# Layer-norm statistics and their Newton step moved from VectorE to ScalarE's running sums, and the batch loop written out

## The reference

```python
xn = (x - mean(x)) / sqrt(var(x) + 1e-5)                 # over the 512 channels
x_dbl = xn @ x_proj_w.T                                  # 128 + 16 + 16 columns: delta, B, C
delta = softplus(x_dbl[:, :128] @ dt_proj_w.T + dt_proj_b)
state = exp(delta * A) * state + delta * B * xn          # 16 states for each channel, along time
s = sum_n(C * state) + xn * D
g = silu(mean over the 2 top experts of relu(xn @ expert_w[e] + expert_b[e]))
out = x + s * g
```

## Time and profile before

| | before |
|---|---|
| median of 3 runs | 2230.43 us (2226.74 to 2242.84) |
| the profiled execution | 2227.24 us, of which the span from first to last instruction 2225.5 us |
| mean granted TensorE clock | 0.949 |
| instructions profiled | 34699 |

### The profile page before, as it was taken

One profiled execution on the slowest core, in us unless ns is written; L12 is line 12 of the kernel. 1 busy time (PEld: TensorE's weight loads), 2 busy tenths in 40 slices (PEclk: granted clock), 3 DMA queues, 4 the chain that ended last, 5 costly groups with the idle time before them and its releaser, 6 DMA issues.

```text
span 2225.5 us, 34699 instructions
## 1 busy us (share of the span) xinstructions
PE 1810.6 (81%) x8688; PEld 1177.6 (53%) x8688; DVE 1962.6 (88%) x3114; ACT 1369.2 (62%) x2370; POOL 1881.8 (85%) x1112
## 2 busy tenths in 40 slices
PE   4597987978789797887969879697896978879886
PEld 2364655545555464555646556365554655546554
DVE  4688899898898988899888998989988898998997
ACT  3456567666566665666565666656665666665664
POOL 2867998888889887898878988788897888988896
PEclk8799999999899999998989999999998999999997
DMA  5869798897969989699797987879888897897995
GB/s 227 287 223 373 231 334 306 255 345 245 355 223 295 330 252 353 222 308 326 244 348 223 324 310 255 328 240 342 276 272 317 256 357 247 295 332 243 374 291 161
DMA packets 279396, 641.23 MB, mean 288 GB/s; under 512 B 22272, under 2 KB 22784, under 8 KB 268944
## 3 DMA queue, kind: packets, MB, share of 16 engines
q1 hardware_dynamic: 185776, 446.36, 57.4%
q10 hardware_dynamic: 68832, 125.34, 15.7%
q0 software_dynamic: 24576, 67.13, 10.9%
HBM read 516.58 MB, written 122.16 MB: 287 GB/s over the span
## 4 chain that ended last, share of the span: by engine, by line
PE 30%; DVE 26%; issue 19%; POOL 10%; ACT 8%; DMA 3%; ACTq 2%; DVEq 1%; SPq 0%; POOLq 0%
PE z_ps L1102 15%; DVE scan_ps L944 11%; POOL dbx L501 6%; DVE p_sb L954 5%; DVE h_sb L944 4%; PE proj_ps L1052 4%; PE y_ps L1118 3%; ACT scan_ps L654 3%; PE y_ps L1135 2%; POOL pp_sb L512 2%; PE xt_ps L1087 2%; DMA c_sb<-bc_rows 2%; PE proj_ps L1078 1%; ACT r_sb L675 1%; ACTq L691 1%
## 5 line engine op out<-in xcount | busy, mean ns | idle before, releaser
L501 POOL TENSOR_TENSOR dbx<-b_sb,u_sb 128x1024 f32<-128x1024 f32 x512 | 1240.8, 2552 | 122.7 <-DMA b_sb<-bc_rows 59.8
L1102 PE MATMUL z_ps<-w_sb,xsT 128*128 128x512 f32 x1920 | 900.4, 613 | 109.3 <-ACT r_sb L675 109.3
L654 ACT ACTIVATE scan_ps<-delta,a_sb 128x512 f32<-128x512 f32 x1024 | 700.1, 690 | 431.1 <-DVE p_sb L954 374.1
L944 DVE TENSOR_TENSOR_SCAN scan_ps<-scan_ps,dbx 128x512 f32<-128x512 f32 x704 | 847.1, 1218 | 104.4 <-ACT scan_ps L654 73.7
L1102 PEld LDWEIGHTS z_ps<-w_sb,xsT 128*128 128x128 f32 x1920 | 356.7, 196 | 490.1 <-issue 474.7
L1118 PE MATMUL y_ps<-ident,p_sb 128*128 128x128 f32 x2816 | 422.8, 284 | 153.8 <-DVE p_sb L954 153.5
L512 POOL TENSOR_TENSOR pp_sb<-h_sb,c_sb 128x1024 f32<-128x1024 f32 (+1 forms) x192 | 410.8, 2139 | 148.2 <-PE y_ps L1135 74.1
L1118 PEld LDWEIGHTS y_ps<-ident,p_sb 128*128 128x128 f32 x2816 | 337.7, 145 | 296.9 <-DVE p_sb L954 212.0
L954 DVE TENSOR_TENSOR p_sb<-scan_ps,c_sb 128x512 f32<-128x512 f32 x704 | 473.5, 673 | 1.3 <-PE y_ps L1118 1.1
L944 DVE TENSOR_TENSOR_SCAN h_sb<-scan_ps,dbx 128x512 f32<-128x512 f32 x320 | 388.1, 1213 | 82.3 <-ACT scan_ps L654 80.5
L669 ACT ACTIVATE xsT<-xt_ps 128x512 f32<-128x512 f32 x240 | 141.7, 590 | 89.3 <-issue 46.5
(11 more groups left out here) (117 smaller groups left out, 1385.7 us busy)
## 6 DMA issues: line engine op xcount, KB each, us to landing
w_sb<-in_ew SPq DMA_DIRECT2D x240, 1024.0 KB, 7.3
b_sb<-bc_rows SPq DMA_DIRECT2D x64, 1024.0 KB, 12.0
ys_rows<-r_sb ACTq DMA_DIRECT2D x240, 256.0 KB, 5.7
xs<-xs_rows ACTq DMA_DIRECT2D x238, 256.0 KB
c_sb<-bc_rows SPq DMA_DIRECT2D x64, 512.0 KB, 14.7
xn<-in_x SPq DMA_DIRECT2D x16, 1024.0 KB, 16.6
c_sb<-bc_rows SPq DMA_DIRECT2D x16, 1024.0 KB, 18.0
xo<-in_x SPq DMA_DIRECT2D x64, 256.0 KB, 8.0
```

What stands on the lines that cost most here:

```text
L501: nc.gpsimd.tensor_tensor(dbx[:, k % DBX_PAIRS], b_sb[:, 2 * m:2 * m + 2, :], u_sb[:, dt % 2, :].unsqueeze(1).to_broadcast([P, 2, T]), ALU ...
L654: nc.scalar.activation(scan_ps[:, bank_of(j), :], delta[:, dt % 2, :], ACT.Exp, scale=a_sb[:, dt, n:n + 1]).then_inc(da_ready, 1)
L944: nc.vector.tensor_tensor_scan(state, bank, dbx[:, j // 2 % DBX_PAIRS, r % 2, :], 0.0, ALU.mult, ALU.add).then_inc(scanned, 1)
L1102: nc.tensor.matmul(z_ps[:], xsT[:, slot, c, :], w_sb[:, i % WRING, c, :], start=(c == 0), stop=False)
```

## The change

For batches 1 to 15 the statistics and the Newton step are made on ACT. Batch 0 keeps its statistics on DVE. For each of the four token tiles an ACT Copy of `xn` onto itself gives the sum of the row as a running sum (`ln_sum`); one small instruction makes the negated mean (`ln_mean`); an ACT Square with the negated mean as its bias gives the sum of squares (`ln_square`; its elements go to `tok`, which holds nothing then). The variance, Ln and Exp follow (`ln_rsqrt`), and then the Newton step and the shift (`ln_step`), where a product of two 128x4 arrays takes four 128x1 instructions, since ACT scales by one value a row. Each stage waits by a semaphore for the one before it. `over_batches` becomes a plain Python loop, so that all 16 batches stand in the program and every semaphore count is a constant.

```diff
-FRONT = {"stats": (2, 3, 4, 5), "var": 5, "root": 8, "apply": (11, 13, 13, 15), "gate": 32, "rank": 38}
+FRONT = {"sum": (0, 1, 2, 3), "mean": 4, "square": (4, 5, 9, 10), "root": 10, "step": (11, 12, 13),
+         "apply": (13, 14, 15, 16), "gate": 32, "rank": 38}
-        def over_batches(eng, body):
-            body(0, 0, 0)
-            body(1, 1, 0)
-            with eng.Fori(1, B // 2 - 1) as i:
-                body(i * 2, 0, i)
-                body(i * 2 + 1, 1, i)
-            body(B - 2, 0, B // 2 - 1)
-            body(B - 1, 1, B // 2 - 1)
+        def over_batches(body):
+            for b in range(B):
+                body(b, b % 2, b // 2)
@@ block.scalar
+            def ln_sum(b, tt):
+                act.wait_ge(x_in, (b + 1) * 16)
+                done = nc.scalar.activation(xn[:, tt, :], xn[:, tt, :], ACT.Copy, accum_out=x_sum[:, tt:tt + 1])
+                if tt == TT - 1:
+                    done.then_inc(ln_act, 1)
+            def ln_mean(b):
+                act.wait_ge(ln_act, ln_no(b, "sum"))
+                nc.scalar.activation(x_neg[:], x_sum[:], ACT.Copy, scale=-1.0 / D).then_inc(ln_act, 1)
+            def ln_square(b, tt):
+                act.wait_ge(ln_act, ln_no(b, "square0") + tt - 1)
+                act.wait_ge(hot_ready, b)
+                nc.scalar.activation(tok[:].rearrange("p t r -> p (t r)")[:, 0:D], xn[:, tt, :], ACT.Square,
+                                            bias=x_neg[:, tt:tt + 1], accum_out=x_sq[:, tt:tt + 1]).then_inc(ln_act, 1)
+            def ln_rsqrt(b):
+                act.wait_ge(ln_act, ln_no(b, "square3"))
+                nc.scalar.activation(x_var[:], x_sq[:], ACT.Identity, scale=1.0 / D, bias=eps[:, 0:1]).then_inc(ln_act, 1)
...
+            def ln_step(b, part):
+                if part == 0:
...
+                    for tt in range(TT):
+                        last = nc.scalar.activation(newt[:, tt:tt + 1], newt[:, tt:tt + 1], ACT.Copy,
+                                                    scale=x_var[:, tt:tt + 1])
+                    last.then_inc(ln_act, 1)
...
             def ln_apply(b, tt):
-                act.wait_ge(bn_done, (b + 1) * 6)
+                if is_first(b):
+                    act.wait_ge(bn_done, 6)
+                else:
+                    act.wait_ge(ln_act, ln_no(b, "shift"))
@@ block.vector
-                        for tt in range(TT):
-                            if j == front["stats"][tt]:
-                                ln_stats(b + 1, tt)
-                        if j == front["var"]:
-                            ln_var(b + 1)
-                        if j == front["root"]:
-                            ln_newton(b + 1)
```

More of the change, by code:

```diff
@@ L34 @@
 DVE_LAG = 7
-FRONT = {"stats": (2, 3, 4, 5), "var": 5, "root": 8, "apply": (11, 13, 13, 15), "gate": 32, "rank": 38}
-FIRST_FRONT = {"stats": (11, 11, 12, 12), "var": 13, "root": 16, "apply": (19, 19, 20, 20), "gate": 37, "rank": 44}
+FRONT = {"sum": (0, 1, 2, 3), "mean": 4, "square": (4, 5, 9, 10), "root": 10, "step": (11, 12, 13),
+         "apply": (13, 14, 15, 16), "gate": 32, "rank": 38}
+FIRST_FRONT = {"sum": (9, 10, 11, 12), "mean": 13, "square": (13, 14, 15, 16), "root": 16, "step": (17, 18, 19),
+               "apply": (19, 19, 20, 20), "gate": 37, "rank": 44}
 XD_AT = {62: 0, 7: 1, 31: 2, 46: 3}
@@ L131, in build @@
         newt = sb("newt", [P, TT])
+        x_sum = sb("x_sum", [P, TT])
+        x_neg = sb("x_neg", [P, TT])
+        x_sq = sb("x_sq", [P, TT])
+        x_var = sb("x_var", [P, TT])
+        three_half = sb("three_half", [P, 1])
         shift = sb("shift", [P, TT])
@@ L572, in batch @@
                         gather_first(b, par, pair, range(TT))
-            over_batches(pool, batch)
+            over_batches(batch)
             for q in (QUADS - 2, QUADS - 1):
@@ L581, in _, with ln_no @@
         def _(act):
+            LN_PARTS = ("sum", "mean", "square0", "square1", "square2", "square3", "var", "log", "root", "root2", "error", "factor", "rstd", "shift")
+            def ln_no(b, part):
+                return 2 + (b - 1) * len(LN_PARTS) + LN_PARTS.index(part) + 1
+            def ln_sum(b, tt):
[3 more added lines that the diff above has]
+                    done.then_inc(ln_act, 1)
@@ new lines, in ln_rsqrt @@
+            def ln_rsqrt(b):
+                act.wait_ge(ln_act, ln_no(b, "square3"))
+                nc.scalar.activation(x_var[:], x_sq[:], ACT.Identity, scale=1.0 / D, bias=eps[:, 0:1]).then_inc(ln_act, 1)
+                act.wait_ge(ln_act, ln_no(b, "var"))
+                nc.scalar.activation(rstd[:], x_var[:], ACT.Ln).then_inc(ln_act, 1)
+                act.wait_ge(ln_act, ln_no(b, "log"))
+                nc.scalar.activation(rstd[:], rstd[:], ACT.Exp, scale=-0.5).then_inc(ln_act, 1)
@@ new lines, in ln_step @@
+            def ln_step(b, part):
+                if part == 0:
+                    act.wait_ge(ln_act, ln_no(b, "root"))
+                    nc.scalar.activation(newt[:], rstd[:], ACT.Square).then_inc(ln_act, 1)
+                    act.wait_ge(ln_act, ln_no(b, "root2"))
+                    for tt in range(TT):
+                        last = nc.scalar.activation(newt[:, tt:tt + 1], newt[:, tt:tt + 1], ACT.Copy,
+                                                    scale=x_var[:, tt:tt + 1])
+                    last.then_inc(ln_act, 1)
+                if part == 1:
+                    act.wait_ge(ln_act, ln_no(b, "error"))
+                    nc.scalar.activation(newt[:], newt[:], ACT.Identity, scale=-0.5,
+                                         bias=three_half[:, 0:1]).then_inc(ln_act, 1)
+                    act.wait_ge(ln_act, ln_no(b, "factor"))
+                    for tt in range(TT):
+                        last = nc.scalar.activation(rstd[:, tt:tt + 1], rstd[:, tt:tt + 1], ACT.Copy,
+                                                    scale=newt[:, tt:tt + 1])
+                    last.then_inc(ln_act, 1)
+                if part == 2:
+                    act.wait_ge(ln_act, ln_no(b, "rstd"))
+                    for tt in range(TT):
+                        last = nc.scalar.activation(shift[:, tt:tt + 1], x_neg[:, tt:tt + 1], ACT.Copy,
+                                                    scale=rstd[:, tt:tt + 1])
+                    last.then_inc(ln_act, 1)
@@ L742, in batch @@
                         store_rows(b - 1, 1 - par, before[j - STORE_LAG + UNITS])
+                    for tt in range(TT):
+                        if j == front["sum"][tt] and nxt:
+                            ln_sum(b + 1, tt)
+                    if j == front["mean"] and nxt:
+                        ln_mean(b + 1)
+                    for tt in range(TT):
+                        if j == front["square"][tt] and nxt:
+                            ln_square(b + 1, tt)
                     if j == front["root"] and nxt:
-                        ln_root(b + 1)
+                        ln_rsqrt(b + 1)
+                    for part in range(3):
+                        if j == front["step"][part] and nxt:
+                            ln_step(b + 1, part)
                     for tt in range(TT):
@@ L793, in batch @@
                     da_unit(b, j)
-            over_batches(act, batch)
+            over_batches(batch)
             copy_y(B - 1, 1, DT - 1)
@@ L970, in _ @@
             nc.vector.memset(acc[:], 0.0).then_inc(acc_zero, 1)
[L971 removed]
+            nc.vector.memset(eps[:], LN_EPS)
+            nc.vector.memset(three_half[:], 1.5).then_inc(eps_set, 1)
             for tt in range(TT):
@@ L1027, in batch @@
                         times_c(b - 1, UNITS - 1)
-            over_batches(dve, batch)
+            over_batches(batch)
             times_c(B - 1, UNITS - 1)
@@ L1181, in batch @@
                             add_y_quad(b - 1, q + QUADS)
-            over_batches(pe, batch)
+            over_batches(batch)
             for q in (QUADS - 2, QUADS - 1):
```

## The result

| | before | changed |
|---|---|---|
| median | 2231.76 us (2226.74 to 2242.84, 4 runs) | 2262.76 us (2258.59 to 2265.41, 4 runs) |
| the profiled execution | 2227.24 us, span 2225.5 | 2265.41 us, span 2263.3 |
| mean granted TensorE clock | 0.949 | 0.941 |

The ratio is 1.013, with a 95% interval of 1.0087 to 1.0173: slower by 1.3%. The prediction said 2250 us, slower by 0.9%.

What follows compares the result with a forecast made beforehand. DVE's and POOL's chains meet at scan 28; from the first relu PE's tiles carry the batch. 2227 - 31 (loop) + 52 (late relu, 14 x 3.7) = 2248, stated as 2250 us; 8-in-10 range 2192 to 2290.

Steps and rivals of the forecast that it cites:

- The loop, -31 us: Batches 3 to 12: writing the loop out saves 3.1 us a batch, 31 us in all.
- The holes: ACT at the loop's five steps back: waits of nearly 5 us put down to "issue", 23.9 us together, would go.
- DVE's work, worth 0: DVE, units 2 to 8: about 5 us a batch removed, counted 0 because POOL's chain sets scan 28.
- Added on ACT, 9.1 us: ACT before the first relu: sums, squares, single steps and small-product groups add 9.8 us, less 0.7 for one `ln_apply`.
- The guess for a running sum: On ACT, each running sum costs a further small instruction, 0.28 less an overlap of 0.09, so 0.19 us.
- The wait for x, 4.4 us on ACT and 3.4 on DVE: Ahead of unit 0: the first sum waits for x, holding ACT 4.4 us and making scan 0 some 3.4 us late.
- The relu 3.7 us late, passed on in full: First relu at 31.9 us against 28.2; the 3.7 us lengthens each of 14 batches, 52 us.
- x in time: Rival: the first sum ahead of unit 0 doesn't stop ACT, leaving the loop's gain, 2196 us; chance 0.23.
- Sums for nothing: Rival: running sums on ACT are free, 6.7 us added, relu 1.3 us late, 2214 us; chance 0.12.
- The loop's gain doesn't come: Rival: removing the loop over batches saves nothing, 2279 us; chance 0.15 shared with dear sums.
- a second pass: Rival, ACT units 0 to 10: sums cost another pass, 13.0 us added, 2302 us; chance 0.15 shared with no loop gain.
- The signs: Profile after: issue holes gone, x heading ACT's waits, relu 28 to 29 us after scan 0, PE's wait longer.

Runs made afterwards that it cites:

- unlooped kernel: The kernel before with its batches written out one after the other, statistics still on VectorE (DVE): 2207.1 us, ratio 0.9886.
- sums later: The changed kernel with the four sums after ScalarE units 3 to 6 instead of 0 to 3, mean and squares moved accordingly: 2240.0 us, ratio 1.0041.
- unlooped, filled: The kernel before with batches written out and TensorE turning tile 2's rows five times instead of once while it waits: 2197.2 us, ratio 0.9838.
- sums of a constant: The changed kernel with ScalarE's four sums reading a constant tile instead of x, so the squares first wait for x: 2203.9 us, ratio 0.9855.
- sums later, filled: The changed kernel with sums after units 3 to 6 and TensorE turning tile 2's rows seven times instead of once: 2210.6 us, ratio 0.9898.
- sums later, small squares: The changed kernel with sums after units 3 to 6 and each square reading 4 columns instead of 512: 2207.5 us, ratio 0.9892.
- changed, filled: The changed kernel with TensorE turning tile 2's rows seven times instead of once while it waits for the first relu: 2242.3 us, ratio 1.0036.
- kernel without statistics: The unlooped kernel with statistics, Newton step and root left out for batches 1 to 15: 2184.5 us, ratio 0.9771.

## Why the prediction was right, and where not

The time was 0.6% above the forecast and on the forecast's side. By steps:

*The loop, -31 us.* Measured -27. The holes are gone, and the batches without it took 133.2 us, not 132.7. By the Trainium skill (Runtime: NRT & Kernel Launch, section Instruction fetch mechanics) fetching a long straight program is mostly hidden, and these runs agree to within that half microsecond a batch.

*DVE's work, worth 0.* Right in the steady part as far as one profile shows: with no statistics at all the batches took 133.5 us against 133.2, or up to 1 us less by the median. Not counted was batch 0, where they lie in the open; there and at the end they are worth some 13 us.

*Added on ACT, 9.1 us.* It is 8.1: four sums at 0.63 = 2.5 (2.8 forecast), four squares at 0.70 = 2.8 (3.0), four single steps 1.1 (1.3), the groups of four 2.4 (2.7), less 0.7. The guess for a running sum, a small instruction at a pitch of 0.19, was nearly twice too much: 0.09 to 0.13. The estimate from the price in the Trainium skill (ScalarE: Activation LUTs, section What ACT_TABLE_LOAD costs), 7.3 us for the lot without a price for running sums, is 0.8 short of the measured, which is about what eight accumulator reads at 0.1 us add.

*The wait for x, 4.4 us on ACT and 3.4 on DVE.* (97.1 - 19.7) / 14 = 5.5 us, and 4.0 us on average in front of scan 0 of batches 2 to 13. Right in kind, 1.1 and 0.6 us short. The 19.7 us of batch 0 were not foreseen: there the sums stood at unit 9, the statistics had stood at unit 11, and x landed at 81.2 us. Batch 0 took 156.3 us, 9.8 more than in the unlooped kernel.

*The relu 3.7 us late, passed on in full.* It came 27.4 + 4.0 = 31.4 us after where scan 0 would have been, 3.2 after the 28.2 of the unlooped kernel; and the batch is 3.8 longer. This is the step that failed, and two errors in it cancel in part. Lateness of the relu by itself is not passed on in full: with the clock held, a relu 1.4 us later (29.6, sums later) made batches 0.6 us longer than the 132.6 of the unlooped kernel with its clock held. For a relu 2.7 us later (30.9, behind 3.5 us of wait for x in front of scan 0) it was 2.2 us more, 134.75, in an execution that lies up to half a microsecond a batch under its median; so there it was most or all of it. And the late relu has a price that I did not list, the halved clock of tile 1. In the earlier trace rows I read PE's wait of 2.14 us as a length only and did not ask what PE does differently after 4.

Both come together in one number, the end of tile 1 after the point where scan 0 would have been (means over batches 2 to 13, with the length of a batch; DVE's wait ahead of scan 0 added to the first):

| kernel | relu | end of tile 1 | batch | slow tiles 1 |
|---|---|---|---|---|
| unlooped, filled | 28.2 | 32.8 | 132.6 | 0 of 12 |
| unlooped | 28.2 | 33.5 | 133.2 | 5 |
| sums of a constant | 27.4 | 33.9 | 133.5 | 11 |
| sums later, filled | 29.6 | 34.2 | 133.2 | 0 |
| sums later, small squares | 28.0 | 34.5 | 133.8 | 12 |
| changed, filled | 30.9 | 35.6 | 134.75 | 0 |
| sums later | 29.6 | 36.3 | 135.9 | 10 |
| changed | 31.4 | 37.8 | 137.0 | 11 |

Up to about 34 us a later end of tile 1 costs at most 0.9 us (132.6 to 133.5); behind it the batch grows about as much as the end is later (34.2 to 37.8, 133.2 to 137.0). That the end of tile 1 is what carries both prices is read from these rows of one execution each, and not tested by itself. What sets the 132.6 us below was not tested either; the kernel without statistics, whose tile 1 ends at 33.0 and whose batches still take 133.5 in its slowest execution, suggests only that neither DVE's statistics nor the relu do.

So of the 58 us of span between the changed kernel and the unlooped one, batch 0 holds 9.8, batches 2 to 13 hold 12 x 3.8 = 46, some 20 of all of it is the clock by the medians with and without the filling (30 by the two profiles), and 5.4 lie ahead of batch 0, below. Batches 1, 14 and 15 together give 3 back. The forecast had 14 equal batches of 3.7 us and nothing outside them; that its 52 us come so near to the 56 measured is in part luck.

*The rivals.* "x in time" would have been right about the price: with x not needed it gave 2204 against its 2196. "Sums for nothing" was right about the sums in units 0 to 3, but not as it was put; they are cheap because ACT has time there where it need not wait for x. "The loop's gain doesn't come" and "a second pass" are out by measurement.

*The signs.* The holes went, and PE's wait grew. The relu came 27.4 us after the late scan 0, not 28 to 29, and the wait for x is second among ACT's waits (97 us, behind 205 for DVE), not first. A pitch of the sums away from 0.7 us was named as a sign of being wrong, and it was 0.63; that moved the forecast's sum by 0.3 us only.

## What to carry to other kernels

Work that goes to an engine with idle time costs nothing only where that engine idles *and* its input is there; here they did so only in part, and both the sums placed too early (a wait for x) and 3 units later (a full ACT) lost what was won. When a change lengthens a wait of PE, read the granted clock behind that wait in every batch before, and price the next tile at 1.2 GHz too. And before a load is moved up on a queue, look for what it waits for there: it is the queue that stands.

## What the runs showed of the hardware that was not expected

- PE's clock after a wait. After 2.14 us of waiting tile 1 ran at half clock in 3 of 14 batches before, in 5 of 14 in the unlooped kernel, with the same wait just ahead of it; in the changed kernel, after 3.7 to 4.9 us in 13 batches and 2.1 in one, in 12 of 14. Eight matmuls then take 5.2 to 6.7 us in place of 3.67. The last wait is not the whole of it: in the kernel without statistics PE stood 3.9 to 4.5 us before its last work ahead of tile 1 and only 1.0 us just ahead of it in batches 2, 6, 9, 12 and 13, and tile 1 ran slow in all five (5.6 to 6.0 us). The Trainium skill (TensorE: Matmul & The Clock Gate, section What's actually happening) has the engine throttled by default and released by activity; the 24 added transposes, after which no tile 1 of 16 was slow, agree with it. What decides a single case stays open.
- The same lead-in code took 5 us more in some executions. Scan 0 of batch 0 starts at 50.5 us in the changed kernel and at 44.9 in the one with the sums later, though both are the same up to there. The fourth group of `proj_ps` matmuls takes 2.61 us in the one and 1.41 in the other:

```profile
32.33 2.61 PE L1120 MATMUL proj_ps<-xwg_sb,xT 128*128 128x168 f32 x8
```

```profile
29.93 1.41 PE L1120 MATMUL proj_ps<-xwg_sb,xT 128*128 128x168 f32 x8
```

  From about 27 us on PE's rows take nearly twice as long in the one as in the other, while the granted clock is given as 1.00 for both. Scan 0 stands at 50.5 to 50.8 us in 4 of the 12 profiles and at 44.9 to 46.0 in the other 8. 5 of the 37.8 us between the profiled spans of before and after are therefore not shown to be the change's.
- A running sum on ACT costs 0.09 to 0.13 us beyond the instruction itself (0.61 and 0.63 against 0.52 between starts, 0.70 against 0.57): its 0.19 us read overlaps what stands beside it.
